# A gated cross-attention and mixture-of-experts kernel: zero rows dropped, the last waits moved to SyncE, and TensorE's expert numbers loaded four at a time

## The reference, cut to what matters

```python
x = x + tanh(g_xattn) * attention(layernorm(x), ctx, mask)      # B=8, S=256, D=512
# attention: scores = q @ ctx.T / sqrt(D), masked softmax over 256 context rows, @ ctx
x = x + tanh(g_ffn) * ffn(layernorm(x))
# ffn: probs = softmax(xt @ w_router.T)   (8 experts), the best 2 kept and renormalised
#      out = sum over the 2 experts of comb * w_down[e] @ (silu(w_gate[e] @ xt) * (w_up[e] @ xt))
#      hidden 512, inner 192, all float32
```

## Time and profile before

| | |
|---|---|
| time, median of 3 runs | 309.64 us (306.84 to 309.8) |
| profiled execution | span 307.2 us from first to last instruction; its own time is not listed, and the median is 2.4 us above the span |
| TensorE busy | 259.1 us (84%), granted clock 0.92 on average |
| VectorE, ScalarE, GpSimd busy | 172.5, 147.3, 164.6 us |
| DMA | 54.72 MB, 178 GB/s mean |
| first phase | to about 138 us |
| second phase | first gather at 139.3 us, last matmul ends at 293.2 us, last scatter issued at 294.8 us |

### The profile page before, as it was taken

The page is one execution under the profiler, slowest core; times in us unless marked ns, Lnnn a source line. Parts: engine busy times, 40 slices in busy tenths (PEclk is TensorE's granted clock), DMA queues, the critical chain, the costliest instruction groups (busy, mean ns, idle before and its releaser), DMA issues.

```text
span 307.2 us, 5562 instructions
## 1 busy us (share of the span) xinstructions
PE 259.1 (84%) x1501; PEld 217.9 (71%) x1501; DVE 172.5 (56%) x649; ACT 147.3 (48%) x310; POOL 164.6 (54%) x152
## 2 busy tenths in 40 slices
PE   1876999999999976357999999999999999999810
PEld 1743876777657745346899999889899999999600
DVE  4552777998986888982244444444444444444400
ACT  2515866865568545121255554444444444444400
POOL 1214574655645436516146786884748647576530
PEclk9995999999999999555799999999999999999965
DMA  7997878678889636304237576785876848868570
GB/s 216 380 404 283 301 254 293 240 266 293 270 289 371 234 106 180 132 2 125 86 68 121 96 141 130 140 143 100 168 141 106 166 87 159 156 113 157 111 97 0
DMA packets 27390, 54.72 MB, mean 178 GB/s; under 512 B 5408, under 2 KB 5536, under 8 KB 27360
## 3 DMA queue, kind: packets, MB, share of 16 engines
q0 software_dynamic: 8304, 19.83, 35.2%
q1 hardware_dynamic: 19056, 34.53, 32.7%
HBM read 33.81 MB, written 20.53 MB: 177 GB/s over the span
## 4 chain that ended last, share of the span: by engine, by line
PE 55%; DVE 16%; DMA 10%; SPq 5%; issue 5%; ACT 4%; POOL 1%; ACTq 0%; POOLq 0%; DVEq 0%
PE S L1069 9%; PE S L1070 8%; PE S L1073 8%; PE A L1059 6%; PE PO L946 3%; DMA out<-X 3%; DMA x2s<-Y 3%; DMA WGl<-in_wgu 3%; DVE TB L722 3%; DVE st L610 2%; DVE X L656 2%; PE S L935 2%; PE PL L1092 1%; PE PO L1097 1%; PE PO L1092 1%
## 5 line engine op out<-in xcount | busy, mean ns | idle before, releaser
L438 POOL DMA_INDIRECT out<-YT,IXI x36 | 56.7, 1576 | 45.1 <-issue 22.4
L1069 PE MATMUL S<-WGh,XTh 128*128 x144 | 52.5, 365 | 1.2 <-ACT XTh L542 1.1
L1070 PE MATMUL S<-WGl,XTh 128*128 x144 | 49.6, 344 | 0.0
L413 POOL DMA_INDIRECT XG<-x2s,IXI x39 | 38.4, 985 | 18.3 <-issue 10.4
L382 POOL TENSOR_TENSOR WGl<-WGl,WGh 128x512 fp32r<-128x512 f32 x24 | 30.6, 1277 | 22.3 <-ACT WGh L506 22.2
L875 DVE TENSOR_TENSOR H<-SG,S 128x192 f32<-128x192 f32 x36 | 12.7, 354 | 49.4 <-ACT SG L549 49.4
L946 PE MATMUL PO<-CX,PT 128*128 128x512 f32 x64 | 33.1, 642 | 6.3 <-ACT PT L477 5.1
L549 ACT ACTIVATE SG<-S 128x192 f32<-128x192 f32 x36 | 11.9, 330 | 51.5 <-PE S L1073 51.5
L373 POOL TENSOR_TENSOR rs<-mv,CS 128x1 f32<-128x1 f32 x32 | 17.6, 551 | 31.8 <-DVE mv L616 31.7
L868 DVE TENSOR_TENSOR XTl<-A,XTh 128x512 fp32r<-128x512 f32 x37 | 25.6, 692 | 15.5 <-ACT XTh L542 15.5
L1073 PE MATMUL S<-WGh,XTl 128*128 x144 | 31.7, 343 | 0.0
(11 more groups left out here) (153 smaller groups left out, 539.1 us busy)
## 6 DMA issues: line engine op xcount, KB each, us to landing
WGl<-in_wgu SPq DMA_DIRECT2D x24, 256.0 KB, 5.0
X<-in_x SPq DMA_DIRECT2D x16, 256.0 KB, 3.7
CT<-in_ctxt SPq DMA_DIRECT2D x8, 512.0 KB, 5.7
CX<-in_ctxn SPq DMA_DIRECT2D x8, 512.0 KB, 5.3
out<-X SPq DMA_DIRECT2D x16, 256.0 KB, 4.6
x2s<-Y SPq DMA_DIRECT2D x16, 256.0 KB, 4.8
WD1l<-in_wd SPq DMA_DIRECT2D x8, 256.0 KB, 4.5
WS<-in_wd SPq DMA_DIRECT2D x8, 256.0 KB, 4.8
```

The lines of the kernel that those rows point to most:

```text
L413: pool.indirect_dma_start(out=XG[:, j % NX, :], out_offset=None, in_=x2s, in_offset=bass.IndirectOffsetOnAxis(ap=IXI[:, j:j + 1], axis=0))\
L438: pool.indirect_dma_start(out=out, out_offset=bass.IndirectOffsetOnAxis(ap=IXI[:, j:j + 1], axis=0), in_=YT[:, j % NB, :], in_offset=None, ...
L1069: pe.matmul(o, XTh[:, j % 2, c, :], WGh[:, bass.ds(e, 1), c, :], start=(c == 0), stop=False)
L1070: pe.matmul(o, XTh[:, j % 2, c, :], WGl[:, bass.ds(e, 1), c, :], start=False, stop=False)
```

## The change

Four edits. (1) The zero rows and everything for them go: `x2s` has 2048 rows, the ten transfers, the memset and the waits on `s_zd` are gone. (2) The gather reads from a second index table `IXG`, which is the token's row or, for an empty slot, row 2047; it is one VectorE instruction, ahead of the two that make `IXI`. The scatter goes on using `IXI` and so the extra rows of `out`. (3) The last waits (all scatters, the last six gathers), with their branches, move from GpSimd's program to the end of SyncE's. (4) TensorE loads expert numbers four at a time, without the bounds check, in rounds 1, 3, ..., 17 and once before round 0; the load stands behind `tx(j+1)` and no longer ahead of it.

```diff
-    x2s = nc.dram_tensor("x2s", [ROWS, DW], fp32, kind="Internal").ap()
+    x2s = nc.dram_tensor("x2s", [T, DW], fp32, kind="Internal").ap()
@@ sync
-            sp.wait_ge(s_z, 1)
-            for i in range(NB):
-                r = slice(T + 128 * i, T + 128 * i + 128)
-                sp.dma_start(x2s[r, :], Z).then_inc(s_zd, 16)
-                sp.dma_start(out[r, :], Z[:, 0:D]).then_inc(s_zd, 16)
@@ sync, at its end
+            live = tiles_of(sp)
+            for i in range(NB):
+                sp.wait_ge(s_add[i], 16 * ((NF + NB - 1 - i) // NB))
+            for j in range(NF, NT):
+                with lives(sp, live, j):
+                    sp.wait_ge(s_add[j % NB], 16 * (j // NB + 1))
+            for j in range(NT - NX, NT):
+                with lives(sp, live, j - NX):
+                    sp.wait_ge(s_g[j % NX], 16 * (j // NX + 1))
@@ gpsimd
-            pool.memset(Z, 0.0).then_inc(s_z, 1)
-            pool.wait_ge(s_ixi, 1)
-            pool.wait_ge(s_zd, 32 * NB)
+            pool.wait_ge(s_ixg, 1)
-                                        in_offset=bass.IndirectOffsetOnAxis(ap=IXI[:, j:j + 1], axis=0))\
+                                        in_offset=bass.IndirectOffsetOnAxis(ap=IXG[:, j:j + 1], axis=0))\
+            pool.wait_ge(s_ixi, 1)
-            landed(NF)
-            for j in range(NF, NT):
-                with lives(pool, live, j):
-                    pool.wait_ge(s_add[j % NB], 16 * (j // NB + 1))
-            for j in range(NT - NX, NT):
-                with lives(pool, live, j - NX):
-                    pool.wait_ge(s_g[j % NX], 16 * (j // NX + 1))
@@ scalar
-                if k == 0:
-                    act.wait_ge(s_zd, 32 * NB)
@@ vector
+            dve.tensor_scalar(IXG[:, :], PC[:, 0:NTP], float(T), float(T - 1), ALU.add, ALU.min).then_inc(s_ixg, 1)
@@ tensor
-            def expert(j):
-                return pe.value_load(ER[0:1, j:j + 1], min_val=0, max_val=E - 1)
+            def experts(j):
+
+                found = nc.values_load_multi_w_load_instructions(
+                    ER[0:1, j:j + 4], engines=[mybir.EngineType.PE], min_val=0, max_val=E - 1,
+                    skip_runtime_bounds_check_because="each is a column number below E, picked by a one-hot product")[1]
+                return {j + i: found[i] for i in range(4)}
-            own, live = {0: expert(0)}, None
+            own, live = experts(0), None
                     gu(j, own[j])
-                    if j + 1 < NF:
-                        own[j + 1] = expert(j + 1)
-                    if 0 <= j - AHEAD < NT - NF:
-                        own[NF + j - AHEAD] = expert(NF + j - AHEAD)
+                    if j + 1 < NT:
+                        tx(j + 1)
+                    if j % 2 == 1 and 2 * j + 2 < NTP:
+                        own.update(experts(2 * j + 2))
                     if j == AHEAD + NT - NF:
                         live = tiles_of(pe)
-                    if j + 1 < NT:
-                        tx(j + 1)
```

More of the change, by code:

```diff
@@ L97, in flamingo @@
         MS = sb("MS", [128, 8, 2, E], bf16)
+        ER = sb("ER", [1, NTP], i32)
         IXI = sb("IXI", [128, NTP], i32)
-        ER = sb("ER", [1, NTP], i32)
+        IXG = sb("IXG", [128, NTP], i32)
         TF = sb("TF", [1, 39])
@@ L118, in flamingo @@
         TB = sb("TB", [128, 4, 128], f32r, where=a)
-        Z = Y2[:].rearrange("p i d -> p (i d)")[:, 0:DW]
         mrow = sb("mrow", [B, S], mybir.dt.uint8, where=a)
@@ L180, in flamingo @@
         s_ws = [sem(f"s_ws{i}") for i in range(NST)]
-        s_z = sem("s_z")
-        s_zd = sem("s_zd")
         s_d = sem("s_d")
@@ L228, in flamingo @@
         s_ixp = sem("s_ixp")
+        s_ixg = sem("s_ixg")
         s_ixi = sem("s_ixi")
```

## The result

The changed kernel takes 295.98 us (median of 4 runs, 294.88 to 297.36) against 309.72 before; the ratio is 0.960 with a 95% interval of 0.955 to 0.965, so 12.5 us less (10.9 to 14.1); the two medians lie 13.7 us apart, which is inside that interval. The forecast was 296.6. The time lies 1.8 us above the span (1.7 to 1.9) in every run here that has both on record, not 2.4 as the prediction took it; by that the profiled execution of before was one of 309.0 us. That of the changed kernel, 297.36 us with a span of 295.5, is the longest of its four.

What follows compares the result with a forecast made beforehand. TensorE was taken as full in the second phase and nearly full in the first, with one hole. Gains of 6.9 + 0.2 + 1.5 + 4.4 = 13.0 us took 309.6 to 296.6 us, range 293.5 to 302.5.

Steps and rivals of the forecast that it cites:

- The place in the queue: First phase: weight unit 1 stood behind 2.64 MB of zeros; without them `pv(1)` starts 5.05 us sooner, 6.9 with the clock.
- Does it last: Rest of the first phase: SyncE's loop through the stores moves with its start, so all 6.9 us are kept.
- The first rival: First phase: SyncE's loop through the stores gives back half of the 6.9 us, 300.1 us; chance 0.15.
- the bounds of 3.4 to 7.5: First phase: range in us for the 6.9 us gain, from half lost to transposes also leaving the low clock.
- The index table: Before the first gather: one VectorE instruction for `IXG` instead of two for `IXI`, gather 0.2 us sooner, bounds 0 to 0.4.
- The loads: Second phase, seven rounds with two expert loads: TensorE's idle time before the transposes goes, 1.5 us less.
- The last rival: Second phase: a load of four is as long as two with checks, gaps stay, 298.8 us; no separate chance given.
- The end: End of the block: without the waits GpSimd's 6.2 us drain starts when the last scatter's issue is over, 4.4 us sooner.
- The second rival: End of the block: GpSimd's drain counts 6.2 us from its DMAs' landing, gain only 1.1 us, 299.9 us; chance 0.16.
- The third rival: Gathers of tiles 36 to 38: all reading row 2047 is slow and delays the last scatters; chance 0.04 mild, 0.02 slower.
- x = 13: Case of 13 us for each gather of tiles 36 to 38, for which the prediction gave 318.0 us.
- The sum: Whole kernel: 6.9 + 0.2 + 1.5 + 4.4 = 13.0 us less, span 307.2 to 294.2.

Runs made afterwards that it cites:

- e3_loads_of_four: The kernel before with only the expert numbers loaded four at a time, unchecked, behind `tx(j+1)`; ratio 0.997.
- e6_one_unchecked: The kernel before with its one or two single loads a round in their old place, but without the bounds check; ratio 0.998.
- e1_no_zero_rows: The kernel before without zero rows and with the gather reading the second index table, last waits and loads as before; ratio 0.974.
- e2_waits_on_sync: The kernel before with only the last waits and their branches moved to the end of SyncE's program; ratio 0.991.
- e8_no_pool_drain: The changed kernel without GpSimd's drain at the end of the block; 294.5 us, ratio 0.957.
- e9_stores_first: The changed kernel with SyncE's weights and stores issued ahead of the load of the next x in each step; 292.4 us, ratio 0.950.

## Why the prediction was right

**The place in the queue.** Right, step by step. The wait of ScalarE went, TensorE was what was late next, `pv(1)` moved by 4.7 us in the profiled execution (5.05 forecast) and by 5.3 in the mean of the traces, and the clock did not fall. Half the zeros gave about half the wait. By the start of `pv(2)` the gain is 7.4 us (33.7 against 26.3 in the means), more than the 6.9 of the sum. Whether the bytes of the zeros or SyncE's time to issue them counts was not separated; the forecast used the bytes.

**Does it last.** This is the term that was off. The prediction took all 6.9 us to the end of the phase, and 0.2 for the index; the traces have 5.8 us at the first gather in the mean, 4.25 in the profiled one. Its reason, "it moves with its start", holds for the kernels with zeros (105.2 to 106.1 us from `pv(2)` on), and for the one with half of them, which starts 2.7 us sooner, but not for those without, which take 107.3 in the mean and vary over 4 us. The whole difference lies between `pv(4)` and `pv(12)`, where SyncE waits for a store to `out` before it loads the next x; ahead of it and behind it the steps take nearly the same time in both. The first rival was right in kind and too dear: 1.7 us are lost in the mean and not 3.5, and in two traces of seven nothing. That the loop through SyncE can set the pace is shown: with the stores first the stretch falls to 103.7 and 103.2, and the waits go. Why the loop is slower and less even when it starts 7 us sooner is not shown. In the mean the bounds of 3.4 to 7.5 held.

**The index table.** 0.2 us for one instruction instead of two was the estimate; the first gather is 0.9 us behind the end of its index in both traces, and the index is one instruction sooner. Too small to be timed.

**The loads.** 1.5 us forecast, 1.6 in rounds 12 to 18 of the profiled execution, 1.3 in `e3_loads_of_four`. Of the 1.6 some 0.4 are round 12's, which varies from 4.1 to 4.7 us over all traces whatever the loads; the other six rounds took 24.7 us before, 23.5 in the changed kernel and 23.6 in both `e3_loads_of_four` and `e6_one_unchecked`. The step "the sequencer runs ahead by enough for one load with its check and not for two" is borne out by two loads without it, which are hidden. One trace does not fit it well: in `e1_no_zero_rows`, with two checked loads and no zeros, the six rounds took 24.0, so beside edits 1 and 2 the loads may be worth 0.5 us and not 1.2. The unknown price, 0.3 to 1.2 us for a load of four, came out at 0.333. The last rival falls.

**The end.** 4.4 us forecast, 4.3 in the trace, 4.2 in `e2_waits_on_sync`. The drain stays 6.2 us long and starts when the issue is over. The second rival, a drain that counts from the landing, falls by the trace. SyncE's end was forecast 1.4 us ahead of GpSimd's and is 2.0 ahead.

**The third rival** costs nothing here, but its mechanism is there. The prediction gave "gathers of tiles 36 to 38 landing later than 5.3 us" as a sign of being wrong, and two of them do in `e8_no_pool_drain` (5.6 and 6.4 us) and one in `e9_stores_first` (5.8); with different rows one does, in `e3_loads_of_four` (5.4). It is far from the 10 us and more at which the queue would have carried it to the end. Two slips of that passage change nothing: at x = 13 its own sum gives 319.0 us and not 318.0, and twice the 4.3 us of the earlier trace rows would be x = 8.6, at which the sum gives 305.8 us, so that "by a factor of two the gathers would stay hidden" does not follow from it.

**The sum.** 13.0 us were forecast and 12.5 measured (10.9 to 14.1). Term by term the profiled execution has 4.25 for 7.1, 1.6 (1.9 with the other rounds) for 1.5, 4.3 for 4.4, and 1.2 that no term had: the low clock at the start of the second phase ended sooner against the work. The prediction named that as a shift of 1 or 2 us either way, and the traces show that this stretch varies by itself. That it filled part of the hole was luck: without it the profiled execution would have gained 10.4 us.

## What to carry to other kernels

Before the first phase of a pipeline, look at what stands in the DMA queue ahead of the first transfer that somebody waits for: here 2.6 MB of zeros, though nobody waited for them, cost 7.4 us at the third tile. A gain at the start of a pipeline is only kept if the loop that follows it has slack, so read that loop first: a queue that waits for the landing of its own store before it issues what others need is one, and changing its order brought 3.4 us at the first gather, while 28 us of waits went from the queue: most of those waits had cost nothing. At the end, see which engine's drain closes the block, and give its waits to an engine that has nothing else to do.

## What the runs showed of the hardware that was not expected

- GpSimd's drain is 0.05 us before any indirect DMA, and 6.2 us after 75 of them, counted from the end of the last issue, whether they had all landed when it began (before) or not (the changed kernel). After 48 and 27 of them it ended 5.0 and 4.9 us behind the last issue, which may in part be a wait for landings.
- A sequencer's load of four values is 0.333 us, of one value 0.306.
- A gather of 128 descriptors that all read the same 2 KB row lands later than one of different rows: 5.1 to 6.4 us against 4.3 to 4.5 for tile 38, in four and five traces. Twelve such gathers have 5.1 us in the mean, fifteen with different rows 4.4.
- In all kernels without any zero rows an undisturbed round of the second phase is 3.91 or 3.92 us, in all with them, half of them included, 3.91 to 3.95, in the mean 0.01 us more. Over 35 rounds that is 0.3 us. What in edits 1 and 2 does it is not shown.
